# One query projection for two groups of heads: rounded rows copied by DMA, the shift in a PSUM bank of its own, a new opening and new order tables

## The reference, cut to what matters

```python
xq = _ada_ln(x_q, t_vec, Wss_q, bss_q)
xkv = _ada_ln(x_kv, t_vec, Wss_kv, bss_kv)
q = (xq @ Wq + bq).reshape(B, Lq, nh, dh)
kv = (xkv @ Wkv + bkv).reshape(B, Lkv, 2, nh, dh)
scores = jnp.einsum('bqhd,bkhd->bhqk', q, k) / jnp.sqrt(jnp.float32(dh))
attn = jax.nn.softmax(scores, axis=-1)
out = jnp.einsum('bhqk,bkhd->bqhd', attn, v).reshape(B, Lq, H)
return x_q + (out @ Wp + bp)
```

## Time and profile before

| what | value |
|---|---|
| median of 3 runs | 445.36 us (443.74 to 445.4) |
| the profiled execution's own time | 443.5 us |
| its span, first to last instruction | 441.7 us |
| TensorE clock granted | 1.00 of full speed |
| PE busy | 429.8 us |
| VectorE busy | 325.1 us |
| ScalarE busy | 212.2 us |
| GpSimd busy | 161.2 us |

### The profile page before, as it was taken

How to read it: one execution, slowest core, us unless ns; L and a number is a source line. 1 busy time by engine, 2 the same in 40 slices (tenths; PEclk the granted TensorE clock), 3 DMA queues, 4 the chain that set the end, 5 groups by cost and what they waited for, 6 DMA issues and landing times.

```text
span 441.7 us, 7170 instructions
## 1 busy us (share of the span) xinstructions
PE 429.8 (97%) x2442; PEld 339.6 (77%) x2442; DVE 325.1 (74%) x833; ACT 212.2 (48%) x376; POOL 161.2 (37%) x241
## 2 busy tenths in 40 slices
PE   8999899999999999999899999999999999999995
PEld 6676556777786587654688988898988988988885
DVE  5987888887788687669866885979477685474772
ACT  2777756765366655634422734444237832134110
POOL 5004527353434300000263424563434434263455
PEclk9999999999999999999999999999999999999999
DMA  7922113012110000000300000010000010001001
GB/s 279 398 81 96 73 49 96 25 47 73 47 27 0 1 0 1 2 0 0 80 0 2 0 1 1 1 47 1 2 0 2 0 50 0 1 0 49 0 1 48
DMA packets 7315, 17.51 MB, mean 40 GB/s; under 512 B 752, under 2 KB 2288, under 8 KB 7152
## 3 DMA queue, kind: packets, MB, share of 16 engines
q1 hardware_dynamic: 6336, 13.84, 8.8%
q0 software_dynamic: 656, 2.29, 2.0%
q10 hardware_dynamic: 288, 0.92, 0.5%
HBM read 14.50 MB, written 2.10 MB: 38 GB/s over the span
## 4 chain that ended last, share of the span: by engine, by line
PE 86%; DVE 7%; ACT 3%; issue 2%; DMA 1%; POOL 0%; POOLq 0%; DVEq 0%; ACTq 0%
PE bank L1294 54%; PE pair L1294 15%; PE pair L1418 4%; PE bank L1460 3%; PE bank L1457 3%; PE bank L1472 1%; PE bank L1426 1%; DMA ctx_sb<-in_ctx 1%; ACT kc L691 1%; PE bank L1483 1%; PE bank L1356 1%; PE bank L1574 1%; ACT xq L745 1%; DVE xq L1052 1%; DVE m_ev L1112 1%
## 5 line engine op out<-in xcount | busy, mean ns | idle before, releaser
L623 POOL TENSOR_TENSOR hs<-hid,hs 128x512 fp32r<-128x512 f32 x48 | 64.1, 1338 | 81.4 <-DVE hs L1212 81.3
L823 ACT ACTIVATE hid<-bank,ab 128x512 f32<-128x512 f32 x56 | 38.4, 688 | 83.9 <-PE bank L1294 62.0
L1294 PE MATMUL bank<-nx,w1h 128*128 128x512 f32 x224 | 71.2, 399 | 0.0
L1294 PE MATMUL pair<-w2h,hs 128*128 128x256 f32 x384 | 70.4, 283 | 0.0
L1042 DVE TENSOR_REDUCE nm<-pair 128x4 fp32r<-128x616 f32 x64 | 51.1, 798 | 15.0 <-PE pair L1418 14.1
L1294 PEld LDWEIGHTS pair<-w2h,hs 128*128 128x128 f32 x384 | 60.3, 189 | 1.4
L1294 PE MATMUL pair<-w2l,hs 128*128 128x256 f32 x192 | 54.1, 282 | 0.0
L755 ACT ACTIVATE pt<-bank 128x512 f32<-128x512 f32 x72 | 40.7, 596 | 25.2 <-PE bank L1294 24.7
L1294 PEld LDWEIGHTS bank<-nx,w1h 128*128 128x128 f32 x224 | 39.9, 189 | 6.9
L1294 PE MATMUL bank<-wh,m_ev 128*128 128x512 f32 x112 | 44.2, 394 | 0.0
L1294 PE MATMUL bank<-nx,w1l 128*128 128x512 f32 x112 | 44.2, 394 | 0.0
(11 more groups left out here) (220 smaller groups left out, 911.6 us busy)
## 6 DMA issues: line engine op xcount, KB each, us to landing
stage<-in_w1n POOLq DMA_DIRECT2D x7, 256.0 KB, 3.2
w1e_sb<-in_w1e SPq DMA_DIRECT2D x1, 1792.0 KB, 8.2
x_sb<-in_x SPq DMA_DIRECT2D x3, 512.0 KB, 10.9
stage<-in_w1a SPq DMA_DIRECT2D x3, 512.0 KB, 11.8
stage<-in_ew2T SPq DMA_DIRECT2D x3, 512.0 KB, 3.9
out_x<-x_sb SPq DMA_DIRECT2D x3, 512.0 KB, 2.6
wss_sb<-in_wss SPq DMA_DIRECT2D x2, 512.0 KB, 7.3
x_sb<-in_x ACTq DMA_DIRECT2D x1, 512.0 KB, 5.0
```

The costliest lines, as they stand in the source:

```text
L623: g_.tensor_tensor(hs[:, q % 3, 1, :], hid[:, (M1 * c + HORD.index(m)) % 2, :], hs[:, q % 3, 0, :], ALU.subtract).then_inc(hl_r, 1)
L823: A(hid[:, n % 2, :], B_H[n % 2][:, :], ACT.Silu, bias=ab1[:, m, c // CPB:c // CPB + 1]).then_inc(h_r, 1)
L1294: ins = mm(dst, a, b_, start=first and i == 0, stop=last and i == len(terms) - 1, skip_group_check=free)
```

## The change

- **Query projection.** Two groups share one: the weights are no longer doubled, `proj(p, k)` runs for GR/2 = 8 pairs, into B_P[0] alone. The bank holds 128 query rows for eight heads, 32 rows (two heads) for each group and s.
- **Layout of xq and kc.** Rows 0-31 hold hi (HI), 32-63 hi again (HI2), 64-95 lo (LO), 96-127 the shift (SHIFT); of the keys hi, lo, hi and ones. The number and shape of the `rows` and `keys` matmuls stay.
- **Who writes what.** ScalarE's `hi(g)` writes HI (two of 32x512). An SP DMA copies HI to HI2 (128 KB) for g > 0, GpSimd does it for g = 0; `rows(g, 0)` waits for it. VectorE's `low(g)` writes LO (two of 32x512) before the shift. The maxima go through a matmul of 32 output rows into B_P[1], and ScalarE's new `shift(g)` copies them to SHIFT, twice 32x512. The next pair's projection waits for both groups' `low`.
- **Keys.** Four key projections of 128 rows in place of eight, `klo` is gone, GpSimd copies the hi rows of kc; the prep steps `("k", t)` are two.
- **Opening.** x's first chunk is loaded in two halves on two queues, both halves of wss ahead of ident and wk; one chain of reciprocal roots for x and context; the context is normalised by ScalarE; the order of the transposes is turned round; 39 warming matmuls in place of 34; GpSimd makes `xkv4`.
- **Order.** EARLY_ORDER and L1_ORDER are new. I is `hi`, J is `low`, Q the key parts, c two steps. SP walks the early list too: it issues its copies and the loaded pieces in that order.

```diff
-PAIR = ((slice(0, 64), slice(64, 128)), (slice(64, 128), slice(0, 64)))
+HI, HI2, LO, SHIFT = slice(0, 32), slice(32, 64), slice(64, 96), slice(96, 128)
+
+
+def pair_rows(g, s):
+
+    r = 64 * (g % 2) + 32 * s
+    return slice(r, r + 32)
...
-        wqh = sb("wqh", (P, KC, NG, P), F32R, l0)
-        wql = sb("wql", (P, KC, NG, P), F32R, l0)
+        wqh = sb("wqh", (P, KC, KC, P), F32R, l0)
+        sb("pad_h", (P, KC, KC, P), F32, l0)
+        wql = sb("wql", (P, KC, KC, P), F32R, l0)
+        sb("pad_l", (P, KC, KC, P), F32, l0)
...
-        nm = sb("nm", (P, 2, TJ, P), F32R, l0)
+        nm = sb("nm", (P, 2, TJ, 32), F32R, l0)
+        sb("pad_n", (P, 2, TJ, P - 32), F32, l0)
...
-        PREP = OPS + [*(("k", gi) for gi in range(NG)), *ANCHOR[0], ("mr", 0), *ANCHOR[1], ("mr", 1), *ANCHOR[2], ("cr",), *ANCHOR[3],
+        PREP = OPS + [("k", 0), ("k", 1), *ANCHOR[0], ("mr", 0), *ANCHOR[1], ("mr", 1), *ANCHOR[2], ("cr",), *ANCHOR[3],
...
         EARLY_ORDER = (
-            "sscVfrPqPfRcVRrPcfPRbfRbcfSRfrKKfKRKPKgRfrPRfA"
-            "SRfKKPRKnKRnfKRPxRSfRA"
-            "fyKfsRKfKRbsKbxSKA"
-            "PPfgKKfRyfRPfnKKRxKRPfnSyA"
-            "RKKuyRKPuzRKyKPRwSzRyxA"
-            "KKRuPKRKuKPRwSzRfssKKA"
-            "RKwPKRKPRfzSRfbA"
-            "RKbfKKPRKwKPRfRgA"
-            "RSfRKKPuRKPunKKSfzKRKuPRnKKwRzKuPRzwSRxA"
-            "RxssKA"
-            "RKwKRPKSKLPKtmRKKA"
-            "RmKRPKRztPSA"
-            "RwKRKuPRKuPRKKzSfRPwKRKuKzRPuKRzKfRSA"
-            "RwKKRlA"
-            "KRKwzNKlSmtKNFKA"
-            "KtCmKKCwWEEA"
-            "CWCmEumzWTTttmwEumWttzmwouttmmtTzTwupmztw"
+            "scsQqfrPPbbfJVIfRfgIcRJfRQQfRQVSPnrfKRKfrKRfKKPRnRIfJA"
+            "SfKbKRfKKIyRKxrRA"
+            "JRsxSRsfKKRbPKfRKgKPRfJnIyA"
+            "SfKKRKfKRnIKxRA"
+            "JRxSRPfyKKRuPyyKRKfzyIKRuSJA"
+            "sKwKRKuzKRKIuRJA"
+            "RswSzRKKPRKPKIbRKwzRfJbSA"
+            "RKgKwKIRKfKRJfRnA"
+            "SRuKKPRKPKnIRKxJRA"
+            "SuzRKKuzRKKuIKRwzRJsxSsA"
+            "KRKmRKtPPRKIKLmtA"
+            "JRfSRwKKRwKRzIKKRfSA"
+            "JRKKPRuKPRIKuKzRwJSfKKRuKzIKRwKRuA"
+            "JRfSRwKlKzRmRtA"
+            "KKRmtSlKzNwKFNKA"
+            "KwCKCKEfEWA"
+            "CCuTmzWtEmtWwuTmEtmzWmwtutmttmzTTuwpzomwt"
         )
...
             load(small[:], "small")
+            sp.dma_start(x[:, 0:2, :], dram["x"][:, 0:2, :]).then_inc(ld_x[0], 16)
             sp.dma_start(wss[:, :, 4:8, :], dram["wss"][:, :, 4:8, :]).then_inc(ld_ss[1], 16)
+            sp.dma_start(wss[:, :, 0:4, :], dram["wss"][:, :, 0:4, :]).then_inc(ld_ss[0], 16)
             load(ident[:], "ident")
             load(wk[:], "wk")
-            sp.dma_start(wss[:, :, 0:4, :], dram["wss"][:, :, 0:4, :]).then_inc(ld_ss[0], 16)
             load(wq[:], "wq")
...
-            for n, (name, i) in enumerate(PE_PIECES):
-                if n == 2:
+            def piece(n):
+
+                name, i = PE_PIECES[n]
+                w = min(512, SHAPES[name][2] - 512 * i)
+                sp.dma_start(stage[2 * (n % 2)][:, :, 0:w], dram[name][:, :, 512 * i:512 * i + w]).then_inc(ld_a[n], 16)
+
+            def prep(n):
+
+                if n == len(OPS) - 1:
                     sp.wait_ge(prep_r, len(OPS))
                     load(w1e[:], "w1e")
-                if n >= 2:
-
-                    pname, pi = PE_PIECES[n - 2]
-                    sp.wait_ge(prep_mm, 1 + PI[("anchor", pi) if pname == "w1a" else ("w2", pi, 1)])
-                w = min(512, SHAPES[name][2] - 512 * i)
-                sp.dma_start(stage[2 * (n % 2)][:, :, 0:w], dram[name][:, :, 512 * i:512 * i + w]).then_inc(ld_a[n], 16)
+                used = [q for q, (name, i) in enumerate(PE_PIECES) if PREP[n] == (("anchor", i) if name == "w1a" else ("w2", i, 1))]
+                if used and used[0] + 2 < len(PE_PIECES):
+                    sp.wait_ge(prep_mm, n + 1)
+                    piece(used[0] + 2)
+
+            def hi(g):
+
+                if g:
+                    sp.wait_ge(qh_r, 2 * g + 2)
+                    sp.dma_start(xq[HI2, g % 2].bitcast(F32), xq[HI, g % 2].bitcast(F32)).then_inc(q2_r, 16)
+
+            piece(0)
+            piece(1)
+            walk(EARLY_STEPS, {"hi": hi, "prep": prep})
...
-                    g_.memset(xq[64:P, g % 2, 0, :].bitcast(F32), 0.0).then_inc(xq_0, 1)
-                    pool.wait_ge(xq_0, 2 * g + 3)
-                    g_.memset(xq[0:64, g % 2, 1, :].bitcast(F32), 0.0).then_inc(xq_0, 1)
-                    pool.wait_ge(xq_0, 2 * g + 4)
+                    g_.memset(xq[SHIFT, g % 2].bitcast(F32), 0.0).then_inc(xq_0, 1)
+                    pool.wait_ge(xq_0, g + 2)
+
+            def key_copy(b, gi):
+
+                pool.wait_ge(kh_r, 2 * (NG * b + gi + 1))
+                g_.tensor_copy(kc[b][LO, gi, :, 0:LK], kc[b][HI, gi, :, 0:LK]).then_inc(k2_r, 1)
+                pool.wait_ge(k2_r, NG * b + gi + 1)
+
+            def parts(gi):
+
+                key_copy(0, gi)
+
+            def prep(n):
+
+                if PREP[n][0] == "k":
+                    for gi in (2 * PREP[n][1], 2 * PREP[n][1] + 1):
+                        key_copy(1, gi)
+
+            def hi(g):
+
+                if g == 0:
+                    for s_ in range(2):
+                        pool.wait_ge(qh_r, s_ + 1)
+                        g_.tensor_copy(xq[HI2, 0, s_, :], xq[HI, 0, s_, :]).then_inc(q2_c, 1)
+                        pool.wait_ge(q2_c, s_ + 1)
+                    pool.dma_start(stage[1][:], dram["w1n"][:, :, 0:256]).then_inc(ld_b[0], 16)
...
             def key_parts(b, gi, src):
 
-                if (b, gi) in KLO_FREE:
-                    act.wait_ge(kg_r, KLO_FREE[b, gi])
-                A(klo[:, gi % 2], src, ACT.Identity, bias=sm("bkl", gi), scale=sm("m1")).then_inc(kg1_r, 1)
-                for s_, (r, low) in enumerate(PAIR):
-                    A(kc[b][low, gi, s_, 0:LK], src[r], ACT.Identity, bias=small[r, SM["bkh"][0] + gi:SM["bkh"][0] + gi + 1],
-                      scale=small[r, SM["m0"][0]:SM["m0"][1]]).then_inc(kh_r, 1)
-
-            def kc_(gi):
-
-                act.wait_ge(k_mm, gi + 1)
-                key_parts(0, gi, key_psum(gi))
+                for s_ in range(2):
+                    r, at = pair_rows(gi, s_), bias_of("bk", gi, s_)
+                    A(kc[b][HI, gi, s_, 0:LK], src[r], ACT.Identity, bias=small[r, at:at + 1]).then_inc(kh_r, 1)
+
+            def parts(gi):
+
+                act.wait_ge(k_mm, gi // 2 + 1)
+                key_parts(0, gi, key_psum(gi // 2))
 
             def blocks(gi):
 
                 act.wait_ge(kc_0, 2)
+                act.wait_ge(kc_1, 2)
                 act.wait_ge(kg_r, gi + 1)
+                act.wait_ge(k2_r, gi + 1)
                 for j in (2, 3):
-                    A(kr[0][:, gi, LK * j:LK * j + LK], kc0[:, gi, 1, 0:LK], ACT.Copy, scale=sm("mkey", j % 2)).then_inc(kk_r, 1)
+                    A(kr[0][:, gi, LK * j:LK * j + LK], kc0[:, gi, 1, 0:LK], ACT.Copy, scale=sm("mkey", j)).then_inc(kk_r, 1)
...
             act.wait_ge(ss_r, 2)
             xt(0, 0)
             xt(0, 1)
-
-            def proj(g, k):
-                if k < KC - 1:
-                    return
-                act.wait_ge(pj_d, g + 1)
-                if g == 0:
-                    act.wait_ge(xq_0, 2)
+            act.wait_ge(cl_t, 1)
+            scaled_context(0)
+            scaled_context(1)
+
+            def hi(g):
+
+                act.wait_ge(pj_d, g // 2 + 1)
                 if g >= 2:
                     act.wait_ge(st_d, (GH + 1) * (g - 1))
-                for s_, (r, low) in enumerate(PAIR):
-                    A(xq[r, g % 2, s_, :], B_P[g % 2][r, :], ACT.Identity,
-                      bias=small[r, SM["bq"][0] + g % NG:SM["bq"][0] + g % NG + 1]).then_inc(qh_r, 1)
+                for s_ in range(2):
+                    r, at = pair_rows(g, s_), bias_of("bq", g, s_)
+                    A(xq[HI, g % 2, s_, :], B_P[0][r, :], ACT.Identity, bias=small[r, at:at + 1]).then_inc(qh_r, 1)
+
+            def shift(g):
+
+                act.wait_ge(nm_d, g + 1)
+                for s_ in range(2):
+                    A(xq[SHIFT, g % 2, s_, :], B_P[1][0:32, :], ACT.Copy).then_inc(sh_r, 1)
...
             stats([(TJ + t, ctxt[0:P if t < 2 else 64, t, :]) for t in range(3)])
-            chain = rsqrt(TJ, 3)
-            for _ in range(4):
-                next(chain)
-            dve.wait_ge(ld_x[0], 16)
-            for j in range(TJ):
-                next(chain)
-                seen = mark(V.bn_stats(st6[:, j, :], x[:, j, :]))
-            for _ in chain:
+            dve.wait_ge(ld_x[0], 32)
+            stats([(j, x[:, j, :]) for j in range(TJ)])
+            for _ in rsqrt(0, TJ + 3):
                 pass
-            dve.wait_ge(dch, seen)
-            for j in range(TJ):
-                aggregated = V.bn_aggr(mv[:, j, :], st6[:, j, :])
-            link(aggregated)
-            x_chain = rsqrt(0, TJ)
```

(84 more changed lines are left out.)

297 lines of the change are left out of this document (158 added, 139 removed).

## The result

The changed kernel takes 441.83 us, median of 13 runs (440.9 to 443.21), beside 443.74 us for the kernel before in the same comparison (13 runs, 443.38 to 445.4). The ratio is 0.9949, 95% interval 0.9936 to 0.9961: 2.3 us faster (0.0051 x 443.7), where 7.5 were forecast. The profiled execution took 442.2 us with a span of 440.1. The kernel before has two groups of run times, 443.3 to 444.0 us with a mean granted clock of 0.997 or more and 444.8 to 445.5 with 0.996 or less, so its median jumps between them: the 445.36 that the forecast started from lies in the second, its profile in the first.

A forecast was written before the change was run, and what follows sets the result against it. VectorE was taken to bound the opening, PE the second stage. Opening -1, PE work -10.0, shortfalls and copy +3.5, second layer 0: -7.5 us, from 445.36 to 437.9; forecast 434.5 to 441.5, with rivals 431.5 to 446.5.

The forecast's parts named there:

- The removed work: Projection and key-projection matmuls: 13.6 us of PE work go, 10.0 of them behind the third av.
- The opening stage: Up to the third av, with VectorE's stream as bound: -1 us, between -4 and +2.
- the sum of the second stage: Where PE sets the pace: -10.0 us of PE work (third stage included), +3.5 for shortfalls and copy.
- the shortfalls: Too little PE work between rows, shift and keys steps: 4.3 us new; with the copy's 1.0, two thirds taken, +3.5.
- About 12 us are waits and pipeline gaps too short for the window rows to show. They stay: Second stage, old order: 150.3 us for 138 of PE work; these gaps remain, only added ones were counted.
- The copy: DMA of the hi rows, awaited at rows(g, 0): lands in 2.0 us, short by 1.0 us in sum.
- the rival: Late copy of the hi rows: gains gone at 3.1 us landing, 455 us at 3.9; 11%.
- Second layer 0: From the first hidden matmul to the end: unchanged, within 1 us of 221.5.
- my term for the third stage: Before the second layer: its PE work lies in the -10.0 us; last wp expected near 208 us.
- The signs of being wrong: Copy 3 us or more, maxima or shift waits up over 6, third av after 68, or second-layer gaps.
- VectorE and ScalarE take over: Second stage becomes a chain of rows, maximum, shift, copy, keys: 443 to 446 us; 14%.
- All of it arrives: The 13.6 us of removed PE work come off whole: 431.8 us; 17%.

The follow-up runs named there:

- a_halfmax: Kernel after, with VectorE's maximum of each score row taken over 77 of 154 keys: 437.24 us, 5.2 us faster than the kernel after.
- a_open: Kernel after, with five opening steps moved so the first queries' rounding and low part come earlier: nothing arrived; first score rows at 24.14 us instead of 24.59.
- b_drop48: Kernel before, with 48 of its 96 projection matmuls left out, order unchanged: 3.9 of 11 us arrived.
- a_drop24: Kernel after, with 24 of its 48 remaining projection matmuls left out: 441.88 us, +0.7 +- 0.9 us against the kernel after.
- a_mt_sp: Kernel after, with the two copies of the second layer's tail keys sent from SP's queue instead of GpSimd's: -2.0 us against the kernel after.
- b_mt_sp: Kernel before, with its two tail-key copies sent from SP's queue instead of GpSimd's: no gain.
- a_shortshift: Kernel after, with ScalarE's 32 shift copies cut from 512 columns to 128: 0.6 or 0.7 us, within the interval of nothing.
- a_nomemset: Kernel after, without GpSimd's 14 clears of the shift rows and TensorE's wait for them: 0.6 or 0.7 us, within the interval of nothing.
- a_drop24_half: Kernel after, with 24 projection matmuls left out and maxima over 77 of 154 keys: the dropped matmuls gave 1.0 +- 1.4 us beyond the shorter maxima.
- a_nocopy: Kernel after, without the 15 DMA copies of the rounded rows and the wait on them: 0.7 +- 1.0 us.
- a_prep: Kernel after, with the second normalisation of two token tiles moved behind the copy of mr: -1.1 us against the kernel after.
- a_cover48: Kernel after, with 48 extra matmuls placed behind the first three score rows of each group: 16.3 us added, 13.8 arrived.
- a_add48: Kernel after, with 48 projection matmuls added back at the first feature half: +9.1 us against the kernel after.

## Why the prediction was right in sign and wrong in size

- **The removed work.** Counted at 10.0 us behind the third `av`; the stage's projections alone gave 10.7. Right as an amount, and taken for a gain.
- **The opening stage** was put at -1 us with the third `av` at 63 to 66; it ended at 65.5, +0.5. VectorE was named as its bound, and the 3.6 us of TensorE work in it gave nothing. a_halfmax ends it 2.5 us earlier, which fits. The first `rows` came 3.1 us later than before; what that cost is not shown, since a_open moved them by 0.45 us only.
- **The first step that failed: the sum of the second stage, -10.0 with two thirds of the shortfalls, +3.5.** It priced the removed work in full and took off only what the new order adds: "They stay, and the question is how many the new order adds". The stage's other steps grew by 7.1 us, twice the 3.5. b_drop48 shows that most of this needs no new order: of 8.3 us taken from the old stage 5.3 came back. The kinds of step that I had counted did come out near their price: `rows` +1.6 (2.1 counted), `shift` +1.8 without the step that changed sides (1.5), `keys` -0.3 beside `mr` (0.7), so +3.1 where +3.5 was booked. What I had put at nothing is the rest. 2.1 us are the wait for `mr`: I looked at the rows, shift and key steps and not at the precompute's, whose bank waits for VectorE in the same way. `wp`, `uz` and the `m` pieces grew by 2.0, of which the remaining kinds gave 0.8 back. The clock's 1.0 us is not a term of its own, it lies in the `keys`, `rows`, `av` and transposes behind `mr`.
- **"About 12 us are waits and pipeline gaps too short for the window rows to show. They stay"** was the assumption under that sum. The kernel stood at the bend, and a_drop24 shows the price of the next removed microsecond as nothing, where my sum was linear with a deduction. PE busy 126.15 of 127 us could not tell this: in b_drop48 it still reads as below, with 36 matmuls (8.3 us) less in the stage.
```profile
65.40:189.40 124.00, 121.40 (x668) 82.24 (x668) 99.07 (x196) 73.19 (x134) 42.52 (x86) 1.00 0.10 29
```
- **The copy** was taken at 2.0 us and landed in 2.3 (2.2 to 2.5); no wait of TensorE is put down to it, and leaving it out gave 0.7 +- 1.0 us. The direction of the rival did not come true; its threshold of 3.1 was not reached. By the fit of the Trainium skill (SBUF — State Buffer, section "The DMA setup-cost knee") an estimate for this size is 2.3 us, and the trace agrees with its 2.3.
- **Second layer 0** was right for its own length (221.5 us both times). **What lies in front of it is the second step that failed**: my term for the third stage held only TensorE's work. The last `wp` came 3.4 us earlier, and 1.9 of it were given back to the tail keys' copy; that it is this copy is shown by a_mt_sp and its control b_mt_sp. The row was in my own list, and I did not ask when it lands and what covers it. Its 3.0 us would have foretold a wait of about 0.4; the other 1.6 are the second copy's last packet behind the instruction packet, 5.0 us to landing and not 3.4, which no row of the kernel before shows.
- Together, in the two traces: opening +0.5 for -1, second stage -3.6 for -6.5 (-10.0 and the +3.5), third stage +1.6 for 0, so -1.5 for -7.5. The medians differ by a little more, -1.9, the ratio by -2.3. The forecast of 437.9 us started from 445.36; from the 443.74 of this comparison it would have been 436.2, so the measured time looks nearer to the forecast than it is.
- **The signs of being wrong** that the prediction named were nearly all absent: the copy took 2.3 us, the third `av` ended at 65.5, the waits that the profile shows for maxima are under 1 us in the stage. Only a gap ahead of the second layer came. The prediction had asked the view of waits, and the growth lies in waits too short for it.
- **Rivals.** "VectorE and ScalarE take over" had the right mechanism for VectorE. Its 443 to 446 us are -2.4 to +0.6 from its start of 445.4, and the measured -2.3 lies at that edge: it came nearer than the forecast, at 14%. ScalarE's part is not seen: a_shortshift. "All of it arrives", -13.6, is ruled out by b_drop48 as well.
- **Open.** What bounds the stage at 120.6 us when maxima are short and matmuls are dropped. What GpSimd's part in VectorE's stretched operations costs over the whole stage: a_nomemset shows it at one place.

## What to carry to other kernels

Before you price removed work, find out on which side of the bend the kernel stands: leave out or add some work of the same kind and compare. Here adding paid 83 to 85% of its length and removing 0 to 35%, while the page said PE 97 and 95%. Walk every step whose bank or buffer waits for the next engine, the rare ones too, and ask of each transfer near a stage's end what covers it once that end moves. Before you read a gain out of two traces, look whether the clock fell in both and how the one transfer landed in each: here these two came to 2.6 us, as much as the whole change.

## What the runs showed of the hardware

- **A short wait counts as busy.** Matmuls of 512 columns that follow each other at 0.23 us are drawn 0.39 to 0.40 us long, so a wait of up to 0.16 us behind one is not idle time in any view. Starts show it.
- **VectorE's operations take longer beside GpSimd's.** The same `lnt` form, from 16 to 190 us, took 485 ns on average before and 605 after; the two key blocks of 128x616 536 and 1077 ns, and 590 in a_nomemset. The groups of the kernel after:
```profile
L954 DVE TENSOR_SCALAR lnt<-x_sb,mv,rs 128x256 f32<-128x256 f32 x16 | 9.0, 605 | 1.2 <-POOL rs L638 0.8 <-PE pair L1631 0.4
L1033 DVE TENSOR_SCALAR keys<-kc,small_sb 128x616 fp32r<-128x616 f32 x2 | 2.2, 1077 | 0.0
```
The Trainium skill (SBUF — State Buffer, section "SBUF: two separate sides") says that the port pair which VectorE's two-port modes share with GpSimd goes to one of the two for a whole instruction. The trace agrees as far as it goes: 1.62 us for the key block is its 0.53 and most of the 1.27 us of the GpSimd operation that began with it, and in a_nomemset, with GpSimd idle, it is 0.53 again. That the port pair is the reason is argued, not shown; by the profile's starts the key block even began 0.01 us ahead of the GpSimd operation.
- **An instruction packet can hold up one packet of a copy, and so the copy.** The second of the two 224 KB copies landed 4.3 to 5.0 us after its issue from GpSimd's queue in the eight traces in which a 16 KB instruction packet ran during it (after, a_drop24, a_drop24_half, a_nomemset, a_nocopy, a_prep, a_open, a_cover48), and 3.4 us in the three without (a_halfmax, a_shortshift, a_add48). TensorE's wait was 1.2 to 2.0 us in the eight and 0.4 in the three. In the kernel before an 8 KB one ended as the second copy was issued, and that copy landed in 3.3 us.
- **The queue of a small copy mattered by its issue.** SP issued the copy 0.03 us after its release and GpSimd 0.60. From issue to landing the first copy took 2.7 to 2.8 us from either queue; the second 3.2 to 3.5 from SP's queue and 3.3 to 3.4 from GpSimd's where nothing held it up. The Trainium skill (DMA: Bandwidth & Descriptors, section "Issuing engine by pattern") has the hardware queues generally faster; these traces don't show it for the landing.
- **The granted clock fell behind a gap, and not every time.** After the 1.9 us of idle time in the kernel after it was 0.57 from 72 to 76 us, and after a gap of 2.0 us in a_drop24_half it was at the lower level for 3.4 us as well. a_drop24 had the same gap (2.0 us) and stayed at 1.00 there, a_halfmax too (1.5 us). The 1.0 us that it costs are therefore not a fixed part of the wait's price, and two traces of like kernels can differ by it.
